# Adding epsilon on the vector engine instead of GpSimd, in the 32 row normalisations of a cross-attention and feed-forward kernel

## The reference

```python
def _layernorm(x, axis=-1, eps=1e-05):
    m = jnp.mean(x, axis=axis, keepdims=True)
    v = jnp.var(x, axis=axis, keepdims=True)
    return (x - m) / jnp.sqrt(v + eps)
...
x = x + _L0_xattn_ref(_layernorm(x, axis=-1), ctx_1024, Wq, Wk, Wv, Wskip)
x = x + _L0_ffn_ref(_layernorm(x, axis=-1), gate_Wq, up_Wq, down_Wq, scales and zeros)
```

## Time and profile before

| | |
|---|---|
| median of 3 runs | 1405.28 us (1405.01 to 1405.45) |
| profiled execution, whole | 1405.51 us |
| its span | 1403.4 us |
| PE busy | 1382.7 us (99%), 6414 instructions |
| DVE busy | 1114.1 us (79%), 1597 instructions |
| ACT busy | 692.6 us (49%), 1284 instructions |
| POOL busy | 309.5 us (22%), 365 instructions |
| granted TensorE clock | 0.999 of full speed |

### The profile page before, as it was taken

How to read it: one execution, slowest core, us unless ns; L and a number is a source line. 1 busy time by engine, 2 the same in 40 slices (tenths; PEclk the granted TensorE clock), 3 DMA queues, 4 the chain that set the end, 5 groups by cost and what they waited for, 6 DMA issues and landing times.

```text
span 1403.4 us, 19583 instructions
## 1 busy us (share of the span) xinstructions
PE 1382.7 (99%) x6414; PEld 676.0 (48%) x6414; DVE 1114.1 (79%) x1597; ACT 692.6 (49%) x1284; POOL 309.5 (22%) x365
## 2 busy tenths in 40 slices
PE   8999998999999999999999999999999999999998
PEld 6676764444444444444444444444444444444443
DVE  6888978887877878878788788788788788787466
ACT  6899984344344444444444444444444444434440
POOL 1132332132122122122212212222212212212200
PEclk9999999999999999999999999999999999999999
DMA  6222222286477576576666756846746746848796
GB/s 189 104 103 87 83 91 61 53 158 121 98 142 127 103 136 115 102 142 112 120 130 112 132 111 115 147 93 125 130 108 122 124 102 124 141 87 151 122 287 274
DMA packets 58982, 174.83 MB, mean 125 GB/s; under 512 B 8000, under 2 KB 11072, under 8 KB 54592
## 3 DMA queue, kind: packets, MB, share of 16 engines
q0 software_dynamic: 34560, 83.90, 38.7%
q1 hardware_dynamic: 24096, 90.20, 21.0%
q10 hardware_dynamic: 288, 0.26, 0.1%
HBM read 73.67 MB, written 100.66 MB: 124 GB/s over the span
## 4 chain that ended last, share of the span: by engine, by line
PE 92%; DVE 4%; ACT 2%; issue 1%; POOL 0%; DMA 0%; DVEq 0%; SPq 0%; POOLq 0%; ACTq 0%
PE ps L592 52%; PE ps L630 9%; PE ps L632 9%; PE ps L631 9%; PE ps L555 3%; PE ps L525 2%; PE ps L802 2%; PE ps L513 2%; PE ps L754 1%; PE ps L550 1%; PE ps L544 1%; ACT temps L879 1%; ACT temps L853 1%; DVE stats L1292 0%; DVE neg_max L1323 0%
## 5 line engine op out<-in xcount | busy, mean ns | idle before, releaser
L592 PE MATMUL ps<-xt,w_gu 128*128 128x512 f16 x3528 | 796.1, 379 | 5.7 <-DVE temps L1539 1.7
L592 PEld LDWEIGHTS ps<-xt,w_gu 128*128 128x128 f16 x3528 | 344.6, 98 | 422.8 <-ACT temps L959 2.6
L992 ACT ACTIVATE stage<-ps,pow 128x512 f32<-128x512 f32 x300 | 204.2, 687 | 320.0 <-PE ps L632 318.3
L1569 DVE SCALAR_TENSOR_TENSOR stage<-ps,pow,stage 128x512 f32<-128x512 f32 x220 | 160.0, 747 | 101.5 <-ACT stage L992 63.2
L630 PE MATMUL ps<-park 128*128 128x512 f16 x560 | 212.2, 379 | 0.0
L631 PE MATMUL ps<-park 128*128 128x512 f16 x560 | 212.2, 379 | 0.0
L632 PE MATMUL ps<-park 128*128 128x512 f16 x560 | 212.2, 379 | 0.0
L439 POOL DMA_DIRECT2D out<-stage x80 | 70.5, 881 | 423.9 <-DVE stage L1569 423.9
L453 POOL DMA_DIRECT2D out<-stage x80 | 69.0, 863 | 297.6 <-ACT stage L992 297.6
L989 ACT CAST park<-temps 128x512 f16<-128x512 f32 x140 | 83.1, 614 | 64.8 <-DVE temps L1553 38.1
L1566 DVE TENSOR_TENSOR park<-temps,park 128x512 bf16<-128x512 f32 x140 | 98.3, 708 | 17.0 <-ACT park L989 14.0
(11 more groups left out here) (140 smaller groups left out, 1620.0 us busy)
## 6 DMA issues: line engine op xcount, KB each, us to landing
out<-stage POOLq DMA_DIRECT2D x80, 512.0 KB, 5.3
out<-stage POOLq DMA_DIRECT2D x140, 256.0 KB, 5.4
grid<-grids SPq DMA_DIRECT2D x136, 256.0 KB, 6.2
raw<-packed SPq DMA_DIRECT2D x34, 512.0 KB, 4.2
out<-stage SPq DMA_DIRECT2D x16, 512.0 KB, 2.7
stage<-x SPq DMA_DIRECT2D x12, 512.0 KB, 3.5
xt<-out SPq DMA_DIRECT2D x12, 512.0 KB, 11.3
out<-xt SPq DMA_DIRECT2D x12, 512.0 KB, 2.6
```

What stands on the lines that cost most here:

```text
L592: mm = pe.matmul(bank, w_gu[e][:, wp, w, P * j:P * j + P], xt[:, xb, xp, j, cols], start=(fresh and n == 0), stop=(n == 3 * J - 1), skip_g ...
L992: return act.activation(dst, ps[:, bank, :], ACT.Copy, scale=pow2[:, 10:11])
L1569: return dve.scalar_tensor_tensor(out=part, in0=ps[:, bank, :], scalar=pow2[:, 10:11], in1=part, op0=ALU.mult, op1=ALU.add)
```

## The change

POOL no longer adds epsilon. DVE does it, directly behind `bn_aggr`, with a 128x1 `tensor_scalar`. That instruction waits for the aggregated statistics (`s_mv`), and for POOL's power of the batch before (`s_rstd`), because `var_eps` has one column for each kind of normalisation. POOL's power waits for `s_eps` alone. The constant column `eps` and its memset go, and the counts of the constants' semaphore are one lower.

```diff
-        eps = sb("eps", [P, 1], F32)
...
-        s_eps = sem("s_eps")
+        s_eps = [sem("s_eps1"), sem("s_eps2")]
...
-            pool.memset(eps[:, :], EPS).then_inc(s_const, 1)
-            pool.wait_ge(s_const, 3)
+            pool.wait_ge(s_const, 2)
...
-            count = [0]
-
             def inverse_deviation(which, b):
-                count[0] += 1
-                par = b % 2
-                wait(pool, s_rstd[which], b)
-                pool.wait_ge(s_mv[which], b + 1)
-                pool.tensor_tensor(var_eps[:, which:which + 1], mv[:, which, par, 1:2], eps[:, :],
-                                   ALU.add).then_inc(s_eps, 1)
-                pool.wait_ge(s_eps, count[0])
-                pool.tensor_tensor(rstd[:, which, par:par + 1], var_eps[:, which:which + 1],
+                pool.wait_ge(s_eps[which], b + 1)
+                pool.tensor_tensor(rstd[:, which, b % 2:b % 2 + 1], var_eps[:, which:which + 1],
                                    neg_half[:, :], ALU.pow).then_inc(s_rstd[which], 1)
...
-            pe.wait_ge(s_const, 4)
+            pe.wait_ge(s_const, 3)
...
                 dve.bn_aggr(mv[:, which, b % 2, :], stats[:, which, :, :].rearrange("p a b -> p (a b)")
                             ).then_inc(s_mv[which], 1)
+                wait(dve, s_rstd[which], b)
+                dve.wait_ge(s_mv[which], b + 1)
+                dve.tensor_scalar(var_eps[:, which:which + 1], mv[:, which, b % 2, 1:2], EPS, None, ALU.add
+                                  ).then_inc(s_eps[which], 1)
```

## The result

| | before | changed |
|---|---|---|
| median | 1405.28 us (22 runs) | 1407.09 us (22 runs) |
| range of the runs | 1404.36 to 1408.08 | 1406.81 to 1408.01 |
| span of the profiled execution | 1403.4 us | 1405.5 us |

The ratio is 1.0013, with a 95% interval of 1.0007 to 1.0019. That is slower by 1.0 to 2.7 us: clear of no change by the interval, and under the 0.2% that I took as measurable. So a difference between medians of different sets is uncertain by some 0.4 us, and I give the loss of each kernel against its own runs of before.

A forecast was written before the change was run, and what follows sets the result against it. PE was taken to set the pace from 48 to 126 us, DVE and ACT nearly full. 0.05 + 0.91 - 0.14 = +0.82 us on 1405.51 gave 1406.3, as a median 1406.1 us; range 1404.6 to 1407.8.

The forecast's parts named there:

- The matmul stage: Everything after 240 us, with no normalisation left; its length was to change by no more than 0.5 us.
- The price c: DVE's time for each new addition behind an aggregation: 0.20 us, 6.4 us over 32, bounds 0.12 and 0.30.
- The middle stretch: Attention steps from 48 to 212 us: late maxima in six even steps make ACT, then PE late, +0.91 us.
- ahead of copying the values out it idles 0.17 us: ACT's last gap in the even steps; PE, waiting for that copy, loses only the lateness over 0.17 us.
- The first stretch: Start to PE's first L544 transpose at 47.87 us: savings at powers against additions on DVE's chain, +0.05 us.
- Its own c lies under that idle time: Batch 0 of the second kind, start-up: DVE sits idle for its power, so the 0.20 us addition costs nothing.
- POOL's library switch takes its place behind the wait for this aggregation: Batch 3, start-up: the switch follows its aggregation; aggregation to power falls from 4.87 to 4.80 us, -0.07.
- The last normalisation: At 218.76 us, where DVE waits 1.00 us for the power, on the chain: -0.14 us.
- (a): Rival: lateness between 48 and 212 us is taken up, only first stretch and end count, -0.09 us, 1405.2; chance 0.30.
- (b): Rival: POOL collisions stretch the new DVE addition to 0.50 us, DVE becomes the bound, +4.4 us, 1409.7; chance 0.04.
- (c): Rival: every addition between 48 and 212 us reaches PE, 5.2 us in place of 0.91, 1410.4; chance 0.03.
- The waits: DVE's waits for POOL's powers over the whole run: to fall from 4.8 us to about 4.0.

The follow-up runs named there:

- one_wait: The changed kernel without the wait for `s_rstd` on the new DVE addition; 1405.82 us against 1405.65 before, ratio 1.0001.
- first_kind: Against the changed kernel, DVE adds epsilon only for the 16 normalisations ahead of attention, POOL for the others; 1405.15 us, ratio 0.9996 to the kernel before.
- second_kind: Against the changed kernel, DVE adds epsilon only for the 16 normalisations ahead of the feed-forward layer, POOL for the others; 1406.04 us, ratio 1.0007 to before.
- moved: The changed kernel with most DVE additions moved away from their aggregations, behind other work, waiting for `s_mv` alone; 1410.85 us, ratio 1.0038 to the kernel before.
- twice: The changed kernel with a second, dependent 128x1 addition behind each first one, into an unread column; 1411.28 us, ratio 1.0039 to the kernel before.

## Why the prediction held, and which of its steps did not

**The forecast as a whole** (no measurable change, a small loss of 0.82 us inside it) had the right sign and the right stage, and was short by 1.0 us. The mechanism held: additions that make the maxima, then ACT, then PE late, past a margin. Its price per addition was too low and its last link was the wrong one. The matmul stage did what was said: the lateness is 2.04 us at the last normalisation and the spans differ by 2.1.

**The price c.** The first step that failed is "c = 0.32 - 0.12 = 0.20 us each". It measured 0.26 with both waits, and 0.31 where the maxima follow, which lengthen by 0.05. I had put the second wait's 0.06 into the upper bound and not into the sum, although POOL's rows had shown it (0.61 for 0.56 us). one_wait shows both: c is 0.19 to 0.20 without that wait, and the loss of the middle stretch falls to 0.68. On POOL's side the second wait shows too: the power starts 0.48 us behind the start of the aggregation at batch 0, and 0.55 at nearly all the others.

**The middle stretch, +0.91 forecast, +1.70 measured.** DVE late by two additions in four even steps and by one in the other two, ACT late by that less the margin, PE late by what exceeds ACT's slack: the mechanism was right, and first_kind, second_kind and one_wait show its threshold. In the order of time I had 0.11, 0.13, 0.14, 0.16, 0.37 and 0 for the six; they measured 0.22, 0.27, 0.27, 0.26, 0.41 and 0.27, the last behind the odd addition. Two terms were wrong. The size: two additions make the maxima's end 0.57 to 0.61 us late where I had 0.40. The link: I named "ahead of copying the values out it idles 0.17 us" and PE's waits for that copy. That wait did not grow (3.2 us, 12 times, before and after). PE is caught earlier in the step, at its L544 transposes, which need the bank that L845 empties. The slack there is about 0.36 us in the first three of the six: 0.53 of lateness less the 0.17 by which L544 itself moved. It is smaller in the next two, 0.15 at 148 us and 0.30 at 173. The group of L544 itself then takes 0.72 us for 0.63, which adds 0.09. one_wait is the measure of what the right price alone would have given: at c = 0.20 the true link passes 0.68 us. That my 0.91, worked out through a link with half the slack, came near it was in part luck.

**The first stretch, +0.05 forecast, +0.42 in the profile**, of which 0.16 is the arrival of `x`. "Its own c lies under that idle time" was wrong for batch 0 of the second kind. That addition stands ahead of maxima on which ACT's next exponentials wait, and DVE, freed 0.63 us earlier by POOL, then ran into ACT and waited 0.34 for it. The changed kernel's timeline of DVE:

```profile
32.25 0.81 DVE L1300 TENSOR_SCALAR park<-stage,mv,rstd 128x1024 f32<-128x1024 f32 x1 [0.85 <-POOL rstd L393]
33.40 0.18 DVE L1359 RECIPROCAL inv_total<-total 128x4 f32<-128x4 f32 x1 [0.34 <-ACT temps L843]
```

Also wrong was "POOL's library switch takes its place behind the wait for this aggregation". In the changed kernel the aggregation of batch 3 came 0.30 us later and POOL's power 0.36 us earlier. The switch back starts behind the all-reduce and took the same time from there (7.53 and 7.56 us), though batch 3's aggregation had moved. The switch to the all-reduce's library starts behind batch 2's power; moved shows it in the large. So PE's first transpose of L544 came at 48.29, later than the 48.1 of the prediction.

**The last normalisation, -0.14 forecast, -0.08 measured** (2.12 to 2.04), the difference being the second wait's 0.07.

**The rivals.** (a), the lateness taken up, did not happen, and not wholly in one_wait either, which still loses 0.68 us in the middle. (b), a collision with POOL that stretches the addition, is out for this change: 153 to 156 ns in all 32. The rule cited from the Trainium skill ("SBUF — State Buffer", "Who interferes with whom") found no partner, as the idle POOL in the earlier trace rows had said. In moved the `tensor_scalar` of the normalisation found one, and took 1.19 us for 0.81. (c), every addition passed on, would have been 5.2 us in the middle stretch and was 1.70.

**The waits** for powers on DVE fell to 2.9 us from the 4.8 of the earlier trace rows, further than the 4.0 forecast.

**A rule read against the rows.** Two instructions on DVE start 0.12 us apart when the second does not wait for the 0.20 us aggregation, and 0.24 when it does. The Trainium skill, page "VectorE: DVE Perf Modes", section "The DRAIN you can't avoid", says that a next operation starts when the pipeline has emptied, or earlier if it is not held, and reports eight chained copies for which the semaphore cost nothing extra. The early start agrees with the 0.12 here. The free semaphore does not carry over to these short instructions: waiting for the aggregation moves the start from 0.12 to 0.24, and the second wait from 0.24 to 0.31, though it is long satisfied. The measurement decides.

**Open:** the odd 0.46 to 0.48 us ahead of one addition in three kernels, behind one of which the changed kernel loses 0.27 us; why the group of L544 takes 0.09 us more when it is late; and why the switch back from the all-reduce took 6.8 to 8.2 us in nine kernels and 10.9 in moved.

## What to carry to other kernels

An instruction of 0.15 us on an engine that is 88% busy is not priced by its own length: count its waits, the overlap that it breaks, and then follow the lateness through each engine's margin until it meets the first buffer that is emptied just in time. Such margins make a threshold, so test the halves of a change apart; here either half alone cost 0.15 and 0.78 us in the stretch where both cost 1.70. And leave out a wait that another instruction on the same engine has already made.

Work taken from an engine that waits 141 us counts only at the few places where somebody waits for it. At one of them, ahead of a slow switch, coming 2.4 us later ended in a loss of 5 us, of which the place in the queue explains 2.3. And a shift in time can bring instructions of DVE and POOL together that had missed each other: look for stretched ones before putting all of a loss down to lateness.

## What the runs showed that was not expected

- A wait that is satisfied long before costs 0.07 us when it is the second on an instruction: on DVE 0.31 or 0.32 for 0.24 us behind the aggregation, at 29 of the 30 places with two waits in the changed kernel (the odd one has 0.66), and at none in one_wait.
- PE loses 0.09 us more over a group of transposes that starts late by 0.17.
- DVE's instruction of 1.22 us took 2.18 us beside a subtraction of POOL's in twice, and two others of 0.69 took 1.53 and 1.54.
- POOL's all-reduce came 5.6 to 5.9 us after the instruction ahead of it ended, in all ten kernels, however long its input had been ready (4.2 us in the kernel before, 6.3 in moved). What stands between the two in the program is the switch of library, so I take this to be its price.
